# A six-block transformer kernel on one core: the tokens between its second and third phase move by GpSimd's indexed transfers

## The reference

```
x = _layernorm(x + _L0_attn_ref(x, ...))       # causal, 16 heads of 16, bias by distance
x = _layernorm(x + _L0_xattn_ref(ctx, ctx, x, mask, ...))
x = _layernorm(x + _L0_ffn_ref(x, ...))        # top 2 of 8 routed experts + 2 shared ones
x = _layernorm(x + _L1_attn_ref(x, ...))       # causal, 16 heads of 16, low-rank projections
x = _layernorm(x + _L1_xattn_ref(x, ctx, mask, ...))
x = _layernorm(x + _L1_ffn_ref(x, ...))        # 256 -> 1024 -> 256, sine and relu
```

## Time and profile before

| | us |
|---|---|
| median of 2 runs | 3683.35 (3681.64 to 3685.06) |
| the profiled execution | 3679.51 |
| its span | 3677.7 |
| PE busy in the span | 3361.8 (91%) |
| DVE | 2627.9 (71%) |
| ACT | 2228.8 (61%) |
| POOL | 1009.4 (27%) |

### The profile page before, as it was taken

One profiled execution on the slowest core, in us unless ns is written; L12 is line 12 of the kernel. 1 busy time (PEld: TensorE's weight loads), 2 busy tenths in 40 slices (PEclk: granted clock), 3 DMA queues, 4 the chain that ended last, 5 costly groups with the idle time before them and its releaser, 6 DMA issues.

```text
span 3677.7 us, 60188 instructions
## 1 busy us (share of the span) xinstructions
PE 3361.8 (91%) x20814; PEld 2507.0 (68%) x20814; DVE 2627.9 (71%) x7168; ACT 2228.8 (61%) x4067; POOL 1009.4 (27%) x1560
## 2 busy tenths in 40 slices
PE   2999999999999838999999999999999874899998
PEld 1777777777777625677777777777777653666665
DVE  5588888888888744667777776777777633688876
ACT  3577767776777632355555555555555543577776
POOL 1144434443444431222222222222222210000000
PEclk8999999999999968999999999999999966899999
DMA  6554446544554221445444444444444412011010
GB/s 188 90 92 88 82 86 106 95 77 84 100 107 70 32 86 34 78 77 92 87 87 91 93 87 92 90 87 93 93 89 80 79 27 80 12 35 34 25 35 23
DMA packets 203405, 283.31 MB, mean 77 GB/s; under 512 B 48929, under 2 KB 131874, under 8 KB 194274
## 3 DMA queue, kind: packets, MB, share of 16 engines
q1 hardware_dynamic: 203106, 279.46, 38.9%
HBM read 179.49 MB, written 96.73 MB: 75 GB/s over the span
## 4 chain that ended last, share of the span: by engine, by line
PE 77%; DMA 6%; DVE 6%; ACT 4%; issue 3%; POOL 2%; SPq 1%; POOLq 0%; ACTq 0%; DVEq 0%
PE ps L816 36%; PE ps L969 10%; PE ps L943 9%; PE ps L983 7%; PE ps L1167 5%; DMA k_stack<-qk_scratch 5%; PE ps L918 2%; PE ps L947 2%; PE ps L1043 2%; ACT pt L1645 1%; POOL pt L1845 1%; PE ps L994 1%; PE ps L957 1%; SPq L1970 1%; PE ps L1053 1%
## 5 line engine op out<-in xcount | busy, mean ns | idle before, releaser
L1645 ACT ACTIVATE pt<-ps 128x512 f32<-128x512 f32 x1280 | 724.1, 597 | 275.4 <-PE ps L969 229.5
L1845 POOL TENSOR_SCALAR_AFFINE_SELECT pt<-pt 128x256 f32<-128x256 f32 x1024 | 390.4, 419 | 905.8 <-ACT pt L1645 905.8
L943 PE MATMUL ps<-k_stack,q_stack 96*128 96x512 f32 (+3 forms) x2048 | 590.8, 348 | 49.8 <-DMA k_stack<-qk_scratch 34.4
L1324 DVE CUSTOM_DVE_ANT_0 ps<-ps,future 128x512 f32<-128x512 f32 (+3 forms) x1024 | 481.7, 514 | 107.5 <-PE ps L943 101.4
L969 PE MATMUL ps<-q_stack,k_stack 100*128 100x512 f32 (+3 forms) x2048 | 534.5, 344 | 15.3 <-ACT pt L1645 10.3
L943 PEld LDWEIGHTS ps<-k_stack,q_stack 96*128 96x128 f32 x2048 | 387.5, 195 | 135.3 <-DMA k_stack<-qk_scratch 40.0
L1317 DVE TENSOR_REDUCE nmax<-ps 128x1 f32<-128x512 f32 (+2 forms) x768 | 359.3, 504 | 118.6 <-PE ps L947 115.5
L969 PEld LDWEIGHTS ps<-q_stack,k_stack 100*128 100x128 f32 x2048 | 346.8, 193 | 87.4 <-ACT pt L1645 34.6
L1851 POOL TENSOR_TENSOR rs<-rs,mhalf 128x4 f32<-128x4 f32 x96 | 97.1, 1012 | 1061.8 <-DVE rs L1360 1060.4
L983 PE MATMUL ps<-pt,v_ones 128*32 128x512 f32 (+3 forms) x4096 | 313.1, 448 | 14.6 <-POOL pt L1845 14.6
L1629 ACT ACTIVATE q_stack<-ps 4x512 fp32r<-4x512 f32 x512 | 261.4, 574 | 52.5 <-PE ps L957 50.0
(11 more groups left out here) (274 smaller groups left out, 7846.7 us busy)
## 6 DMA issues: line engine op xcount, KB each, us to landing
qk_scratch<-parts SPq DMA_DIRECT2D x64, 1024.0 KB, 6.2
q_stack<-qk_scratch SPq DMA_DIRECT2D x384, 128.0 KB, 6.3
k_stack<-qk_scratch SPq DMA_DIRECT2D x384, 128.0 KB, 6.8
gate_of<-gate_scratch SPq DMA_DIRECT2D x128, 256.0 KB, 6.3
x_mid<-x_ring SPq DMA_DIRECT2D x32, 512.0 KB, 4.1
x_ring<-x_mid SPq DMA_DIRECT2D x32, 512.0 KB, 4.7
x_ring<-in_x SPq DMA_DIRECT2D x16, 512.0 KB, 3.9
out_dram<-x_ring SPq DMA_DIRECT2D x16, 512.0 KB, 2.9
```

What stands on the lines that cost most here:

```text
L943: done = e.matmul(bank(bank_of[piece])[:, at:at + width], a.q[0:96, base + h, t * P:(t + 1) * P], a.k[0:96, base + h, 0:width], start=True ...
L1324: done = e.tensor_tensor_reduce(src, src, future[:, SEQ - width:SEQ], -1.0, 3e38, ALU.add, ALU.min, nmax[:, g % 2, u // 5 * 2 + h, t:t + 1])
L1645: e.activation(dst, src, ACT.Exp).then_inc(exp_up.sem)
L1845: done = e.affine_select(out=blk, in_=blk, compare_op=ALU.is_ge, fill=0.0, base=0, pattern=[[0, 2], [1, P]], channel_multiplier=-1)
```

## The change

The stores of phase 2 (`st 2`) and the loads of phase 3 (`ld 3`) leave SP. In their place POOL issues indexed transfers: `sc` scatters the tokens of a sequence to the rows of `x_mid[1]`, and `ga` gathers them from there. Each is four instructions, one for each of a partition's four tokens, and each of these moves 128 rows of 1 KB, whose numbers stand in a table `row_ids` (128 x 64 integers), loaded by one more transfer in phase 1's prologue. The rows lie where the plain transfers had them. The pieces' times in `TABLE` are the same, now in POOL's list. A sequence's four transfers count on one semaphore (`x_spread` or `x_picked`), and the next user of the tokens waits for all four. The loads of phase 2 stay on SP and now wait for `x_spread`; the gathers of phase 3 wait for SP's stores of the output.

```
-            "st 2": [298.553],                      # sync, phase 2
+            "sc 2": [298.553],                      # gpsimd, phase 2
-            "ld 3": [-34.372],                      # sync, phase 3
+            "ga 3": [-34.372],                      # gpsimd, phase 3
...
-                first = [("ld", ph, b) for b in range(RING)] if engine == "sync" else []
+                mine = {1: ("sync", "ld"), 2: ("sync", "ld"), 3: ("gpsimd", "ga")}[ph]
+                first = [(mine[1], ph, b) for b in range(RING)] if engine == mine[0] else []
...
+        x_spread = [signal(f"x_spread{k}", "gpsimd", "sc", TT, 16, lambda key, k=k: key[1] % RING == k) for k in range(RING)]
+        x_picked = [signal(f"x_picked{k}", "gpsimd", "ga", TT, 16, lambda key, k=k: key[1] % RING == k) for k in range(RING)]
...
+        row_ids = sb(ctx, "row_ids", [P, BATCH * TT], I32)
...
+                elif kind == "sc":
+                    b = key[1]
+                    e.wait_ge(*ln_up["a1", b])
+                    for t in range(TT):
+                        at = bass.IndirectOffsetOnAxis(ap=row_ids[:, b * TT + t:b * TT + t + 1], axis=0)
+                        e.indirect_dma_start(x_rows[:, :], at, x_ring[:, b % RING, t, :], None).then_inc(
+                            x_spread[b % RING].sem, 16)
+                elif kind == "ga":
+                    b = key[1]
+                    if b >= RING:
+                        e.wait_ge(*x_out[b % RING][3, b - RING])
+                    for t in range(TT):
+                        at = bass.IndirectOffsetOnAxis(ap=row_ids[:, b * TT + t:b * TT + t + 1], axis=0)
+                        e.indirect_dma_start(x_ring[:, b % RING, t, :], None, x_rows[:, :], at).then_inc(
+                            x_picked[b % RING].sem, 16)
...
+                        e.dma_start(row_ids[:, :], dram["row_ids"]).then_inc(small_in, 16)
...
-                        e.wait_ge(*x_out[b % RING][ph, b - RING])
+                        e.wait_ge(*(x_out if ph == 1 else x_spread)[b % RING][ph, b - RING])
```

More of the change, by code:

```diff
@@ L74 @@
 ENGINES = ("tensor", "scalar", "vector", "gpsimd", "sync")
-TAGGED = ("ld", "st", "tc", "tb", "tm", "ln", "lm", "bk")
+TAGGED = ("ld", "st", "sc", "ga", "tc", "tb", "tm", "ln", "lm", "bk")
 class Signal:
@@ L377, in pieces_of @@
         put("lm", "a" + layer, b)
-        put("st", ph, b)
+        put("st" if ph == 1 else "sc", ph, b)
     if ph == 1:
@@ L412, in pieces_of @@
     else:
-        put("ld", 3, b)
+        put("ga", 3, b)
         put("cw", b)
@@ L466, in decoder @@
         x_mid = [scratch(f"x_mid{n}", (BATCH, P, TT, DIM)) for n in range(2)]
+        x_rows = x_mid[1].rearrange("b p t d -> (b p t) d")
         kt_scratch = scratch("kt_scratch", (P, 2, CT, BATCH * CTX))
@@ L777, in tokens @@
                 return att[layer].o[:, :, :], o_up[b + layer * BATCH, GROUPS - 1]
-            ready = {"a0": x_in[b % RING][1, b], "ex": x_in[b % RING][2, b], "x1": x_in[b % RING][3, b]}.get(tag)
+            ready = {"a0": x_in[b % RING][1, b], "ex": x_in[b % RING][2, b], "x1": x_picked[b % RING][3, b]}.get(tag)
             if ready is None:
@@ L1200, in vector @@
                                                 ALU.subtract).then_inc(ctx_parts)
-                                e.wait_ge(small_in, 80)
+                                e.wait_ge(small_in, 96)
                                 e.tensor_scalar(xk_b[:, :], xk_b[:, :], SCALE, None, ALU.mult).then_inc(bias_up)
@@ L1927, in sync @@
                     elif ph == 2:
-                        e.wait_ge(small_in, 112)
+                        e.wait_ge(small_in, 128)
                     else:
@@ L1932, in sync @@
                     for k in range(RING):
-                        e.wait_ge(*x_out[k][key[0], BATCH - RING + k])
+                        e.wait_ge(*(x_spread if key[0] == 2 else x_out)[k][key[0], BATCH - RING + k])
                 if kind in ("prologue", "end"):
@@ L1941, in sync @@
                     if b >= RING:
-                        e.wait_ge(*x_out[b % RING][ph, b - RING])
-                    src = dram["x"][b].rearrange("(t p) d -> p t d", p=P) if ph == 1 else x_mid[ph - 2][b]
+                        e.wait_ge(*(x_out if ph == 1 else x_spread)[b % RING][ph, b - RING])
+                    src = dram["x"][b].rearrange("(t p) d -> p t d", p=P) if ph == 1 else x_mid[0][b]
                     e.dma_start(x_of(b), src).then_inc(x_in[b % RING].sem, 16)
@@ L1947, in sync @@
                     tag = ("x0", "a1", "ff")[ph - 1]
-                    dst = out[b].rearrange("(t p) d -> p t d", p=P) if ph == 3 else x_mid[ph - 1][b]
+                    dst = out[b].rearrange("(t p) d -> p t d", p=P) if ph == 3 else x_mid[0][b]
                     e.wait_ge(*ln_up[tag, b])
@@ L2032, in lay_out @@
     qkv = a["L0_attn_Wqkv"].T
-    out = {"x": a["x"], "trig": trig_tables(), "w4": rows_of(a["L0_xattn_wk_w"])}
+    out = {"row_ids": np.arange(BATCH * SEQ, dtype=np.int32).reshape(BATCH, P, TT).transpose(1, 0, 2).reshape(P, -1).copy(),
+           "x": a["x"], "trig": trig_tables(), "w4": rows_of(a["L0_xattn_wk_w"])}
     ctx = a["ctx_1024"].reshape(BATCH * CTX, DIM).T
```

## The result

The changed kernel takes 3731.76 us (median of 2 runs, 3728.6 to 3734.93), where the kernel before took 3683.35: a ratio of 1.013, with a 95% interval from 1.0088 to 1.0175. The forecast was 3719 us, in a range from 3680 to 3795.

The account below looks back on a forecast made before the run. PE's list was taken to bound phases 2 and 3. Phase 2's 30 us, phase 3's 5 and the boundary's 1 made 36 on a span of 3677.7, with measuring offsets 3719 us, range 3680 to 3795.

Parts of the forecast that it names:

- PE's list is the clock: Phases 2 and 3: PE, 97% and 96% busy, sets the pace, so a push on PE stays in the time.
- Phase 2, 4t - 2.7 for each sequence: Scatters ahead of POOL's gate product push PE by 2.3 us in each of 13 sequences, 30 us in all.
- 4t - 0.66: Phase 2: how much later POOL's gate product starts behind four scatters, as it was free to start 0.66 us later.
- The cover on ACT: Phase 2: ACT, busy with `q_stack`, takes `hid_h` 1.60 us after the gate product ends, hiding that much delay.
- The last piece of cover: Phase 2: 0.43 us between DVE's reduction freeing a PSUM bank and PE beginning new scores in it.
- The size of t: Time one indexed issue holds POOL, taken as 1.25 us, near the gate product; about 100 us on the sum per us.
- Phase 3, 4t + L - 6.8: Gathers push PE 0.4 us in each of 12 sequences, 5 us; L, last issue's end to rows landed, 2.2 us.
- The boundary: Between phases 2 and 3: later last store +4.4, no loads ahead of context -1.8, faster context -1.5; sum +1 us.
- Hidden: Rival: t at most 0.7 or push made up, all covered, only the boundary left; 3680 to 3688 us, chance 0.22.
- Slow issue: Rival: an indexed issue takes 1.65 us or more, over 2% slower; decided at t = 1.6; chance 0.27.
- Late landing: Rival: POOL's transfers land only after 6.8 us, phase 3 costs 60 us, 3779 in all; chance 0.03.
- Held by DVE: Rival: phase 3's eight `tr<-ang` on DVE hold up indexed issues, 5 to 20 us, 3724 to 3739; chance 0.10.

Follow-up runs that it names:

- e9: Changed kernel with one more POOL power, result unused, between the power and the four gathers of phase 3's last 12 sequences; 3739.84 us, one execution.
- e4: Changed kernel with one indexed issue of 4 KB rows per sequence in place of four, in both phases; 3678.32 us, ratio 1.000.
- e8: Kernel before, with SP issuing phase 3's first four token loads behind the prologue's context, masks and weights, not ahead; 3672.56 us, ratio 0.998.
- e3: Changed kernel with one number changed, so POOL issues phase 2's four scatters behind the gate product, not ahead of it; 3691.2 us, ratio 1.0047.
- e10: Changed kernel with two unused DVE additions of 128 x 1024, both inputs in SBUF, behind `rs<-ag,rs` in phase 3; 3746.5 us, one execution.
- e12: Changed kernel with two unused one-input DVE copies, 128 x 512 then 128 x 2304, behind `rs<-ag,rs` in phase 3; 3753.78 us, one execution.
- e5: Changed kernel with phase 3's loads back on SP and phase 2's store as eight indexed issues of 512-byte rows; 3813.25 us, ratio 1.0365.

## Why the prediction was right, and where it was off

**PE's list is the clock.** Right. Every push that reached PE stayed in the time, in phase 2 and in phase 3, and no other engine made it up.

**Phase 2, 4t - 2.7 for each sequence.** The mechanism was right and so was nearly all of its size. From the first scatter to the gate product it is 4.87 us (2171.66 to 2176.53), the scatters start 0.26 us later behind the power than SP's store did, and 0.66 us of it was free before: 4.47 us. My 4t - 0.66 at t = 1.25 was 4.34. The cover on ACT is the 1.60 us that I took. The last piece of cover I put at the wrong place: PE is stopped at the bank that DVE's `parts` frees, 5 us ahead of the scores' bank which I named, and it has 0.46 us to spare there, not 0.43. So 2.4 us of push by the rows, 2.5 of wait in the profile, 2.7 in the period: the difference of 0.2 I did not trace. The term was 30 us; it measured 36.4, of which 13 x 2.7 is 35, and one dip of the clock 1.4. That there was one dip only is luck: with the four to eight of the other profiles the term is 39 to 47 us.

**The size of t.** I chose it by the power and the gate product of POOL, and it came out within 0.02 us. The reasoning was thinner than the result: what it took for one price is 0.96 us of instruction and 0.30 of gap, and I had argued with 128 addresses. That 1.25 came so near is luck, as the sum moves by 100 us for each us of it. No run here changed the number of rows in an issue, so whether rows have a price stays open; bytes have none.

**Phase 3, 4t + L - 6.8.** Right in kind and half the size: 5 us against 9.2. L was 2.1 and not 2.2, t 1.27, with no pause behind the last issue; by these alone the push would be 0.2 us. The other 0.38 us of each sequence is the longer first gather, 0.32 of it DVE's hold (1.33 us against the 1.01 of `e9`), and 2 us more are two late landings.

**The boundary.** The sum of +1 measured +2.6. From the first scatter of the last sequence to the context's issue it is 10.2 us (3072.99 to 3083.15) in place of 4.6: +5.6 where I had +2.6. The rows of the last scatter are in 1.5 us after its issue, not 2.2; 3.8 us more pass from there to the context's issue, against 0.7 in `e4`, and I had nothing for that piece. What holds the barrier there I did not trace. For the transfers' new order I took -1.5, and at PE's first product it is 1.2 (20.6 us against 21.8). The reason that I gave, that the weights come behind in the same queue and the tokens still move, is what the table shows; `e8`, where the tokens are behind the weights, has 3.9 there, and 1.8 from the earlier issue. The rest is -0.5 behind PE's first product and -1.3 ahead of the first scatter, in the stretch that goes with the clock. As this stretch alone varies by 12 us from profile to profile, the +2.6 proves little; the 3.9 us from the first scatter to the first transposition (63.6 against 59.8) come again in `e3` and `e9` to `e12` (63.7 to 64.6).

**The rivals.** Hidden: fell with t, and `e4` shows what it would have been, 3678 us at a ratio of 1.000. (That no POOL instruction takes less than 0.4 us holds for the groups of the earlier trace rows; memsets at the kernel's start last 0.1.) The rule of the Trainium skill (DMA: Bandwidth & Descriptors, section "Anatomy of one DMA — SWDGE (gpsimd) path") that the generation of descriptors is small is not borne out for issues with an index: 1.27 us from one to the next. Its fixed 2 us until the receipt agree with the 2.1 us that the last gather takes to land. Slow issue: decided at 1.6 us, measured 1.27; `e5` shows how steep that side is, 133 us above the kernel before for 10 us of hold. Late landing: 2.1 us, not 6.8. Held by DVE: the mechanism is there, at 0.32 us for each of 11 sequences, 3.5 us in all, just under the 5 to 20 that I gave; I had looked at the wrong instruction. The eight `tr<-ang` of a period leave the issues at 0.94 to 0.98 us. The box of the Trainium skill on the "DVE blocks DMA" trap (SBUF — State Buffer) agrees with the one long copy of `e12`; the two-input instructions, which hold an issue as well, it doesn't mention, but the Trainium skill's GPSIMD Engine Reference, section "8. Key points", names them beside the fast modes.

**What no term had.** The clock that falls while PE waits. In the changed kernel it is 1.4 us in one period, in the one with eight issues 1.8 us in every period. The other piece is the time between the last scatter's landing and the context's issue, above.

## What to carry to other kernels

Before transfers are moved to POOL, count the issues and not the bytes, and look at the piece that stands next in POOL's list: the same 64 scatters cost 36 us ahead of a product that others wait for, and nothing at all behind it. Four issues of 128 rows that lie side by side in memory can be one issue with longer rows, which left both phases' periods as they were. And at a phase's beginning all transfers that the chain waits for, here the context and the weights, go first, and the tokens that are read 50 us later go behind them: tokens issued by another engine at the same time took the gain back.

## What the runs showed of the hardware

- An indexed issue of 128 rows holds POOL for 0.96 us, the first after a pause for 1.01 to 1.06, and two in a row are 1.27 us apart, for rows of 512 bytes and of 1 KB; with 4 KB rows one lasts 0.94 to 1.06 us where DVE does not hold it. A plain one holds POOL for 0.56 us, and SP for 0.33.
- DVE instructions with two inputs in SBUF hold up POOL when they meet an issue near its start: an issue of 0.96 us took 2.91 beside one of 2.29 and ended 0.8 us after it. They hold up a power too (1.51 us in place of 1.01). A one-input copy of 1.35 us held an issue near its end: 2.25 us, 0.13 us beyond the copy.
- TensorE's granted clock fell to 0.50 in a wait of 7.6 us in every period (+1.8 us each), and at a wait of 2.5 us in 29 of 78 cases of six profiles (+1.4 us each), each time out of a stretch at 1.00.
- The last weights of a phase were in 15.4 us after the context's issue with 2 MB of tokens behind them in the queue, 19.3 with the tokens ahead, and 18.1 to 21.2 with the tokens issued by POOL at the same time.
